# Sixteen-head attention on one Trainium2 core: head outputs as single 128-row products, with new fixed orders

## The reference, cut to what matters

```
scores = einsum("bhqd,bhkd->bhqk", q, k) / 4
scores = scores * mask - 10000 * (1 - mask)      # self, cross; l3: -inf where masked
probs  = softmax(scores)
heads  = einsum("bhqk,bhkd->bhqd", probs, v)
out    = heads.reshape(b, s, 256) @ w_o
```

## Time and profile before

| | |
|---|---|
| median of 3 runs | 1013.15 us (1012.09, 1013.15, 1017.78) |
| profiled execution: span from first to last instruction | 1009.9 us |
| PE busy | 944.2 us, 93% |
| PE weight loads | 755.1 us, 75% |
| DVE, ACT, POOL busy | 729.8 us (72%), 568.3 us (56%), 537.1 us (53%) |
| mean granted PE clock | 0.993 of full speed |

### The profile page before, as it was taken

The page is one execution under the profiler, slowest core; times in us unless marked ns, Lnnn a source line. Parts: engine busy times, 40 slices in busy tenths (PEclk is TensorE's granted clock), DMA queues, the critical chain, the costliest instruction groups (busy, mean ns, idle before and its releaser), DMA issues.

```text
span 1009.9 us, 27529 instructions
## 1 busy us (share of the span) xinstructions
PE 944.2 (93%) x10944; PEld 755.1 (75%) x10944; DVE 729.8 (72%) x1607; ACT 568.3 (56%) x1320; POOL 537.1 (53%) x662
## 2 busy tenths in 40 slices
PE   7969999987979999999999999999999998999997
PEld 4758887765747877878877788786767776788885
DVE  1585466798998788865656764687889798977665
ACT  2587742432334654777666677635646553576572
POOL 0664353574674467665156633474666665665332
PEclk9999999999979999999999999999999999999999
DMA  8401420000001001001101001101001000000001
GB/s 302 169 2 46 181 58 1 2 1 2 2 1 34 2 3 28 14 2 55 31 18 46 5 2 30 51 2 27 2 17 27 3 1 2 14 14 2 14 1 44
DMA packets 28589, 31.71 MB, mean 31 GB/s; under 512 B 14736, under 2 KB 25264, under 8 KB 27824
## 3 DMA queue, kind: packets, MB, share of 16 engines
q1 hardware_dynamic: 27440, 28.12, 8.8%
q10 hardware_dynamic: 1024, 1.85, 0.5%
HBM read 27.86 MB, written 2.10 MB: 30 GB/s over the span
## 4 chain that ended last, share of the span: by engine, by line
PE 64%; DVE 13%; DVEq 7%; issue 5%; ACT 4%; POOL 4%; POOLq 1%; DMA 1%; ACTq 0%; SPq 0%
PE bank L506 8%; PE bank L494 8%; PE bank L378 7%; PE bank L399 7%; PE bank L366 7%; PE bank L391 5%; DVE lane L1013 3%; PE bank L457 3%; PE bank L481 3%; DVEq L1016 3%; PE bank L524 2%; PE bank L535 2%; PE bank L438 2%; DVE bank L1009 2%; DVEq L1010 2%
## 5 line engine op out<-in xcount | busy, mean ns | idle before, releaser
L1423 POOL TENSOR_TENSOR lane<-lane 128x512 f32<-128x512 f32 x160 | 166.0, 1044 | 163.7 <-DVE lane L887 95.7
L1189 ACT COPY lane<-bank 128x512 f32<-128x512 f32 x232 | 132.1, 588 | 139.9 <-PE bank L366 92.5
L366 PE MATMUL bank<-ident,lane 128*128 128x128 f32 x896 | 131.8, 279 | 9.0 <-POOL lane L1423 3.7
L366 PEld LDWEIGHTS bank<-ident,lane 128*128 128x128 f32 x896 | 101.7, 141 | 34.4 <-issue 10.5
L1495 POOL TENSOR_TENSOR lane<-lane 128x512 f32<-128x512 f32 x64 | 80.9, 1269 | 54.6 <-DVE lane L1013 54.2
L1157 ACT ACTIVATE lane<-lane 128x256 f32<-128x256 f32 x96 | 52.4, 594 | 61.6 <-POOL lane L1408 61.1
L1013 DVE TENSOR_TENSOR_SCAN lane<-lane,bank 128x256 f32<-128x256 f32 x128 | 80.9, 673 | 4.7
L885 DVE TENSOR_REDUCE lane<-lane 128x8 f32<-128x512 f32 x96 | 64.7, 674 | 23.0 <-ACT lane L1208 22.0
L1171 ACT ACTIVATE lane<-bank,vecs 128x256 f32<-128x256 f32 x112 | 55.5, 551 | 40.4 <-PE bank L366 40.1
L1485 POOL TENSOR_TENSOR lane<-lane 128x512 f32<-128x512 f32 x40 | 46.9, 1180 | 45.2 <-DVE lane L993 45.2
L1208 ACT ACTIVATE lane<-lane 128x512 f32<-128x512 f32 x96 | 59.7, 631 | 11.6 <-DVE lane L865 11.3
(11 more groups left out here) (161 smaller groups left out, 2206.3 us busy)
## 6 DMA issues: line engine op xcount, KB each, us to landing
lane<-in_inT SPq DMA_DIRECT2D x16, 256.0 KB, 4.5
lane<-in_x SPq DMA_DIRECT2D x16, 256.0 KB, 3.4
w_d<-in_w_d SPq DMA_DIRECT2D x1, 3072.0 KB, 11.6
w_am<-in_w_am SPq DMA_DIRECT2D x1, 2048.0 KB, 13.5
lane<-in_inT SPq DMA_DIRECT2D x16, 128.0 KB, 2.9
lane<-in_ctx SPq DMA_DIRECT2D x8, 256.0 KB, 2.8
out_x<-lane SPq DMA_DIRECT2D x8, 256.0 KB, 2.3
w_c<-in_w_c SPq DMA_DIRECT2D x1, 1792.0 KB, 10.4
```

The source lines that it names most:

```text
L366: ins = pe.transpose(t[:, i * P:(i + 1) * P], src, ident[:, :])
L1189: s.copy(out, src).then_inc(bk.free_sem(key), 1)
L1423: p.tensor_tensor(q, q, den.unsqueeze(2).to_broadcast([P, n, 512 // n]), ALU.mult).then_inc(sig["normal"].sem, 1)
```

## The change

The head outputs of self, cross and l3 are made as products with 128 rows. The probabilities are ordered so that the two batch halves (sequences h = 0 and h = 1 of a token tile) take the outer half of a score bank. After the transposition the two heads of a pair lie on partitions 0 to 63 and 64 to 127, for one sequence. `va` becomes block-diagonal: 32 columns per pair, the even head's values on the upper 64 partitions and the odd head's on the lower 64, zeros elsewhere. One product then gives both heads, without accumulation.

- `weighted` makes 16 products, into one bank; `v_heads` copies 128x256 once per `weighted` in place of 128x128 twice.
- The values are copied in four pieces of 64x256: two by ACT (h = 0) and two by DVE (h = 1, new function `v_values`, a new step in DVE's stream), and the bank of v has two takers. Both wait for a new signal that POOL has cleared `va` (`CLEARED`).
- POOL clears the whole of `va` (128x1024) for self and for cross in place of 128x256 gaps; l3 reuses the zeros of cross.
- PE waits for the copied values ahead of the first `weighted`, no more ahead of `scores`.
- `cross_c` moves into the input region, two small areas move, the arena grows by 64 columns.
- The strings `ORDER` (DVE has 24 more steps) and `BANKS` (960 in place of 1008 entries) are made anew. Most steps of PE move by a few places; SP now issues the inputs, masks and x of all lanes ahead of the l0 MLP weights, which are its 17th step of 60 and were its 11th.

```diff
-ARENA = 7044
+ARENA = 7108
+SMALL_AT = 7044
+PW = 2 * D
+CLEARED = {"self": 2, "cross": 3, "l3": 3}
-                self.va = lane.at(va, TT * NH // 2, VW).rearrange("p (t n) e -> p t n e", t=TT)
+                self.va = lane.at(va, G * NH // 2, PW).rearrange("p (h t n) e -> p h t n e", h=2, t=TT)
+                self.cleared = lane.arena[:, va:va + G * NH // 2 * PW]
+        def by_batch(ap):
+            return ap.rearrange("p (h n k) -> p h n k", h=2, k=S)
+        def head_values(key, A, h, r):
+            src = bk.tile(key)[S * h:S * h + S, :].rearrange("p (n r d) -> p n r d", r=2, d=D)[:, :, r, :]
+            return A.va[S * r:S * r + S, h, :, :, D * r:D * r + D].rearrange("p t n d -> p (t n) d"), src
...
-                                o = t[j][S * i:S * i + S, m * T:(m + 1) * T].rearrange("p (r h k) -> p r h k", r=2, h=2)[:, :, h, :]
+                                o = t[j][S * i:S * i + S, (2 * h + m) * P:(2 * h + m + 1) * P]
...
             def weighted(c):
+                if c == 0:
+                    pe.wait_ge(bk.free_sem((g, tag, "v")), bk.taken_at((g, tag, "v")))
                 for j in (2 * c, 2 * c + 1):
                     pe.wait_ge(bk.free_sem((g, tag, "probsT", j)), bk.taken_at((g, tag, "probsT", j)))
-                keys = [(g, tag, "heads", c, h) for h in range(2)]
-                t = [pe_open(pe, key) for key in keys]
+                key = (g, tag, "heads", c)
+                t = pe_open(pe, key)
                 for i in range(TT):
-                    for r in range(2):
+                    for h in range(2):
                         for n in range(4):
-                            m, j = n % 2, 2 * c + n // 2
-                            for h in range(2):
-                                q, blk = slice(h * S, (h + 1) * S), (2 * m + r) * P + i * S
-                                ins = pe.matmul(t[h][32 * n:32 * n + 32, i * S:(i + 1) * S], A.va[q, i, m * PT_ + j, D * r:D * r + 2 * D],
-                                                A.probsT[q, slot(j), blk:blk + S], start=(r == 0), stop=(r == 1))
-                                if (i, r, n) == (TT - 1, 1, 3):
-                                    ins.then_inc(bk.full_sem(keys[h]), 1)
-
-            for key in [(g, tag, "q"), (g, tag, "k", 0), (g, tag, "k", 1), (g, tag, "v")]:
+                            m, j, b = n % 2, 2 * c + n // 2, 2 * i + h
+                            at = (2 * h + m) * P + i * S
+                            ins = pe.matmul(t[32 * n:32 * n + 32, b * S:(b + 1) * S], A.va[:, h, i, m * PT_ + j, :],
+                                            A.probsT[:, slot(j), at:at + S], start=True, stop=True)
+                ins.then_inc(bk.full_sem(key), 1)
+
+            for key in [(g, tag, "q"), (g, tag, "k", 0), (g, tag, "k", 1)]:
...
+        def v_values(v, g, tag, A):
+            key = (g, tag, "v")
+            v.wait_ge(lane(g).sig["masks"].sem, lane(g).sig["masks"].at(g, CLEARED[tag]))
             v.wait_ge(bk.full_sem(key), bk.full_at(key))
+            for r in range(2):
+                out, src = head_values(key, A, 1, r)
+                ins = v.tensor_copy(out, src)
+            ins.then_inc(bk.free_sem(key), 1)
...
             for c in range(2):
-                for i in range(2):
-                    v_heads(v, g, tag, c, i, A.headsT[:, c, i::2, :], VALUE_BIAS[tag])
+                v_heads(v, (g, tag, "heads", c), c, A.headsT[:, c, :, :], VALUE_BIAS[tag])
                 yield
...
         def s_values(s, g, tag, A):
             key = (g, tag, "v")
-            s_copy(s, key, values(A.va.rearrange("p t n e -> p (t n) e")), bk.tile(key)[:, :].rearrange("p (n r d) -> p n r d", r=2, d=D))
+            s.wait_ge(lane(g).sig["masks"].sem, lane(g).sig["masks"].at(g, CLEARED[tag]))
+            s.wait_ge(bk.full_sem(key), bk.full_at(key))
+            for r in range(2):
+                out, src = head_values(key, A, 0, r)
+                ins = s.copy(out, src)
+            ins.then_inc(bk.free_sem(key), 1)
...
-            p.memset(L.self.va[:, :, :, D:2 * D], 0.0)
+            p.memset(L.self.cleared, 0.0).then_inc(sig["masks"].sem, 1)
...
-            p.memset(L.cross.va[:, :, :, D:2 * D], 0.0)
+            p.memset(L.cross.cleared, 0.0).then_inc(sig["masks"].sem, 1)
```

## The result

The changed kernel takes 1025.14 us (median of four runs, 1022.50 to 1028.02) beside 1014.32 for the kernel before: ratio 1.0108, 95% interval 1.0084 to 1.0131. It is slower by 1.1%, where 1006.5 us was forecast. Its profiled execution has a span of 1025.9 us and a mean granted PE clock of 0.978 (before: 1009.9 and 0.993).

What follows compares the result with a forecast made beforehand. PE was taken to bound most of the kernel, DVE 200 to 325. -8.8 (products) - 0.4 (waits) + 1.7 + 1.0 (DVE) = -6.5 us: span 1009.9 to 1003.4, forecast median 1006.5 us, range 995 to 1021.

Steps and rivals of the forecast that it cites:

- The saving on PE: Head products: 0.20 us saved per call, 44 calls counted outside 200 to 325, -8.8 us; shorter PE waits, -0.4 us.
- The rival in which the loads do not overlap: Head products: with one row group, stationary loads stand beside products, a call takes 0.94 us, total 1022.7 us; chance 0.03.
- DVE's value copies: Two new 64x256 copies per attention on DVE, 413 ns each, 0.76 us for the pair.
- inherited: Rival: DVE's queue takes over ACT's waits for the values product, 200 to 425 and 725 to 875; 1021.5 to 1028 us; chance 0.15.
- +2.7 us for DVE's work: DVE's net added copying where it is full: +1.7 us between 200 and 325, +1.0 us between 725 and 875.
- ACT ... Nothing: Values copy on ACT: +0.18 us per attention, 4.4 us in all, covered by 139.9 us idle ahead of that line.
- POOL's clearing "nothing": Clearing of 1024 columns on POOL: 0.95 us each, 10.3 us more busy time, counted at nothing, with 2 us in the range.
- The orders made anew: Weave of lanes on all engines: no term in the sum, called impossible to price step by step.
- 66 to 69 was the condition: Sign: if PE's idle total over the kernel stays near 66 to 69 us, the sum is right.
- the new orders close gaps as well: Rival: a quarter of PE's 29.6 us idle in 200 to 325 and 725 to 875 goes, -7.4 more, 999 us; chance 0.17.
- DVE's busy time: Sign: DVE's busy time over the whole kernel would be about 741 us.
- The recorded bound of 16 us for the net DVE cost: Upper bound on DVE's net added busy time over 24 attentions, estimated at 11.5 us, lower bound about 5.

Runs made afterwards that it cites:

- e5: The kernel before with half of its head products left out (the odd head of each pair), orders, banks, copies and waits unchanged: 1003.9 us, ratio 0.9903.
- e6: The lean version in the old orders: e3 with POOL clearing 64 columns instead of 1024 and ACT copying only two value pieces: 1003.7 us, ratio 0.9901.
- e11: e2 with only two of the four value copies on ACT, the full clearing kept: 1015.3 us, ratio 1.0018.
- e2: The changed kernel in its new orders, with all four value copies on ACT and none on DVE: 1022.2 us, ratio 1.0078.
- e3: The changed code in the orders of the kernel before, with all four value copies on ACT: 1015.4 us, ratio 1.0011.
- e9: The lean version e6 in the new orders (two value copies on ACT, clearing of 64 columns): 1013.5 us, ratio 1.0016.
- e13: e9 with 65 products that nobody reads, ahead of the 23 steps where PE idled over 1 us: 1005.7 us, ratio 0.9920.
- e7: The changed kernel with 154 products that nobody reads, ahead of the 25 steps where PE idled over 1 us: 1021.4 us, ratio 1.0081.
- e8: The kernel before with 62 products that nobody reads, ahead of the 11 steps where PE idled over 1 us: 1012.8 us, ratio 0.9996.
- e14: The kernel before with 28 products that nobody reads, ahead of the same 11 PE steps as in e8: 1010.1 us, ratio 0.9957.
- e12: The changed kernel with 69 products that nobody reads, ahead of the same 25 PE steps as in e7: 1018.9 us, ratio 1.0059.

## Why the prediction was wrong, point by point

**The saving on PE: right in size, and in what it is worth with what goes along.** A call takes 0.58 us (forecast 0.58 to 0.60), and the lean version in the old weave is 10.0 us faster (-8.8 - 0.4 forecast for PE). That all of PE's time outside 200 to 325 counts is not borne out: e5 was paid half of its 19 us. At that rate the shorter calls would bring about 5 of the 10.0 us. That the whole came out near the forecast is in part luck: the rest came with what e6 changes beside PE.

The rival in which the loads do not overlap gave a call of 0.94 us, and 0.58 refutes it at that price. The rule of the Trainium skill (TensorE: Matmul & The Clock Gate, The mechanism) is that a weight load overlaps running products only when its row group differs. The trace does not agree with the price that the rival worked out from it. But an instruction of the new call takes 18 ns (0.58 / 32) where one of the old call takes 12 (0.79 / 64, and 0.39 / 32 in e5). Whether loads are a part of these 6 ns no run shows.

**DVE's value copies: the busy time right, its price too small.** 427 ns against 413, and the waits for the product are 1.5 us, so they are not inherited. But the sum had +2.7 us for DVE's work, in the stretches where DVE is full: +3.8 for the value copies (3 x 0.76, and half of 4 x 0.76) and -1.1 for the head copies. Two copies on DVE for each attention cost 9.1 us (e11 to after), for 20.5 us of busy time: 44% of it, where I had counted a quarter of the 11.5 us net. The chains fit this: e11's page has DVE and its queue at 27%, the changed kernel's at 34%.

```profile
PE 59%; DVE 18%; DVEq 9%; ACT 5%; issue 4%; POOL 4%; POOLq 1%; DMA 1%; ACTq 0%; SPq 0%
```

(This is e11's line; PE had 48% in the changed kernel's.)

**"ACT ... Nothing" and POOL's clearing "nothing": a wrong step of method, not tested at its own size.** I took idle time ahead of a line as cover. In the version with four copies, ACT's additional 48 copies of 0.365 us, 17.5 us under 139.9 us of idle time, cost 6.1 to 7.0 us. The changed kernel's own ACT work grows only by two copies of 365 ns in place of one of 588, 3.4 us in all, and no run prices those 3.4 us. The clearing is 952 ns as forecast. It costs 4.2 us in the old weave and 0.2 in the new one, which is not apart from nothing: in the changed kernel, nothing, as said.

**The orders made anew, priced at nothing: the step that failed.** The forecast said "I am wrong above all if the weave of the lanes ... moves PE's idle time by more than the products save". It does: PE's idle time is 82.8 us where 66 to 69 was the condition, 17.1 more than before where the products save 8.8. The sum had no term for the orders. The same work is 6.8 us (e2 over e3) to 11.6 us (e9 over e6) dearer in the new ones.

How much of this is waiting, and how much the half-rate clock after it, is not settled. For the clock: 9.7 us come back once the gaps of e9 are partly filled (e13). Against it as the main part: filling brings the kernel before 4.4 us too, the lean version in the old orders was not filled, and before and after stay 8.6 us apart at equal half-rate time (e7, e8). The profiled executions of e6 and e9 point to the waits: PE is busy 934.6 and 934.8 us, idle 67.4 and 76.6, at clocks of 0.993 and 0.983, so nearly all of the 9.4 us between them is idle time of PE. The rival "the new orders close gaps as well" had the wrong sign: there are 25 gaps over 1 us in place of 11.

The account, in us, by the ratios and 1013: lean version in the old orders -10.0; new orders +11.6; clearing +0.2; two copies on DVE +9.1. That is +10.9, the ratio 1.0108. The steps are differences along one chain of runs (before, e6, e9, e11, after), so their sum proves nothing; each step is a price in its place. As to the clock: half-rate time is 23.7 us higher than before, and over 173 runs, within each kernel, the span rises by 0.34 us (standard error 0.02) for each us of half-rate time (a slope fitted over all of them). Taken as a cause that would be some 8 us of the 10.9, an estimate and a correlation. The filled kernels give as much per us of half-rate time (e13: 30 us less, 9.7 us faster; e14: 10 us less, 4.4 us faster), but the comparison of e7 with e8 leaves the clock 2.3 us of the difference, plus what the 92 added products cost, which is not measured.

**DVE's busy time: 759.0, forecast 741.** The head copies save 3.9 us (e3: 725.9 against 729.8; I had 6.7, with 0.14 us a call for l3 too, where its rows give 0.08), the value copies add 20.5, and the new orders add 12.3 (e2 738.2 against e3 725.9) without one instruction more. (The recorded bound of 16 us for the net DVE cost is 14 with the overlap that its other terms have.) In the old orders, e3's and e6's, L1097's group is at 499 ns, in the new ones at 671 (e2), 695 (e11, and after). Two DVE instructions of L1000 and POOL's products beside them, in time order (DVE, then POOL):

```profile
695.90 2.73 DVE L1000 SCALAR_TENSOR_TENSOR lane<-lane,vecs 128x256 f32<-128x256 f32 x2
```

```profile
694.01 4.34 POOL L1525 TENSOR_TENSOR lane<-lane 128x512 f32<-128x512 f32 x3
```

DVE takes 1.37 us for each where the median is 484 ns, while POOL takes 1.45 for each where its mean is 1.30. PE waits for it 2.8 us (L619). Of the 48 instructions of L1097 and L1000 in the changed kernel, the 29 beside which POOL runs no product take 488 ns at most; the 19 that meet one take up to 1.49 us. The Trainium skill (SBUF — State Buffer, Who interferes with whom) says that a DVE instruction with two SBUF inputs contends with a GpSimd instruction that reads SBUF; this trace agrees. These two groups hold 8.8 us more than before. What that cost was not measured by itself: an order in which they do not meet was not tried.

**What stays open.** Why the new orders have the longer gaps: between 285 and 303 us the scans of one lane are held up by a reduction of another (0.9 us), but no run moves single steps of the order, nor `BANKS` or SP's order by themselves. And how the new orders' price divides between waits and clock: e6 with its gaps filled, beside e13, would tell more.

## What to carry to other kernels

Price a new instruction order like any other part: take the longest idle places of the leading engine, and not only its idle total, and look at its clock after each. Idle time ahead of a line is no cover for more work on that line if the next engine waits for its result; here 35% to 44% of the added busy time of the copies (ACT and DVE) came out as span, and of POOL's clearings a third in one order and nothing in the other. When a change mixes new work with a new order, run the new work in the old order with the side work stripped: that one run (e6) showed that the idea without its side work was worth 1.0%; e9 to e11 showed what took it back.

## What was not expected of the hardware

- Work that nobody reads, put where PE would have waited, made three kernels faster: by 0.96% (e13 to e9), 0.48% (e12 to after) and 0.43% (e14 to before). Twice as much was worse than half in the kernel before (0.9996 against 0.9957), and no better in the changed one.
- A microsecond at the half-rate level went with 0.34 us of span, not 0.5 as it would if PE's work alone set the time.
- A DVE instruction of 484 ns (L1000, two inputs in SBUF) lasts up to 1.48 us while POOL runs a product of two SBUF operands, and POOL's own lasts 1.45 instead of 1.30 us. The mean of L1078 (L1097 after the change) goes from 498 to 695 ns by the order.
- A copy's time goes by its columns: 64 partitions with 256 columns take 427 ns on DVE, where 128 partitions with 256 columns take 413 (L870), and 365 ns on ACT, where an instruction on 128 partitions with 256 columns took 385.
